# A two-layer adapter kernel on one core: new order of all engines within a step, and gathers put between the stores

## What is computed

```python
def cond(x, A, B, ids):                       # both layers
    Bx = einsum('bni,bri->bnr', x, B[ids])
    return einsum('bnr,bor->bno', Bx, A[ids])
# layer 0: c = cond(x, A0, B0, itok_B_3_7)
# x = x + c @ W0.T + b0 + sum_e alpha_e(c) * 2 * (c @ loraA_e.T) @ loraB_e.T
# layer 1: c = cond(x, A1, B1, itok_B_4_50)
# x = x + c @ W1.T + b1 + sum_e gate_e(c) * 2 * (c @ A_e.T) @ Bm_e.T
```

## Time and profile before

| | |
|---|---|
| median of 3 runs | 334.89 us (334.2 to 335.64) |
| profiled execution, its own time | 334.41 us |
| its span in the trace | 332.7 us |
| mean granted PE clock | 0.995 of full |
| PE busy | 307.0 us, 92% |
| DVE, ACT, POOL busy | 220.1, 186.4, 63.3 us |
| DMA | 56.16 MB, 169 GB/s mean |

### The profile page before, as it was taken

How to read it: one execution, slowest core, us unless ns; L and a number is a source line. 1 busy time by engine, 2 the same in 40 slices (tenths; PEclk the granted TensorE clock), 3 DMA queues, 4 the chain that set the end, 5 groups by cost and what they waited for, 6 DMA issues and landing times.

```text
span 332.7 us, 6476 instructions
## 1 busy us (share of the span) xinstructions
PE 307.0 (92%) x2048; PEld 284.4 (85%) x2048; DVE 220.1 (66%) x476; ACT 186.4 (56%) x384; POOL 63.3 (19%) x58
## 2 busy tenths in 40 slices
PE   5994998799989998999979999999999999999894
PEld 4453998589978998999979999999999999899783
DVE  2156887686738766686658666777668676864556
ACT  1446976946546565755466465646575657461520
POOL 5600000620042103320143003320332024200000
PEclk9999899999999999999999999999999999999999
DMA  7999973006870388126840587037811783041006
GB/s 267 345 365 381 347 208 156 0 8 167 300 224 0 104 243 302 51 60 212 286 139 0 158 284 250 2 103 244 299 47 55 255 292 92 0 193 62 1 0 252
DMA packets 30773, 56.16 MB, mean 169 GB/s; under 512 B 3633, under 2 KB 20050, under 8 KB 30754
## 3 DMA queue, kind: packets, MB, share of 16 engines
q1 hardware_dynamic: 29666, 52.97, 48.3%
q0 software_dynamic: 1088, 2.97, 2.5%
HBM read 39.15 MB, written 16.78 MB: 168 GB/s over the span
## 4 chain that ended last, share of the span: by engine, by line
issue 41%; PE 20%; DMA 13%; POOL 12%; DVE 6%; ACT 3%; SPq 2%; POOLq 1%; DVEq 0%; ACTq 0%
POOL xs_lo L952 8%; DMA out<-xraw 6%; DMA xraw<-x_in 6%; PE ps_d L307 3%; PE ps_d L309 3%; PE ps_d L308 3%; POOL a1s_lo L952 2%; DVE xs_lo L740 2%; DVE xraw L942 2%; PE ps_d L545 1%; PE ps_p L307 1%; PE ps_d L547 1%; ACT res L574 1%; SPq L253 1%; SPq L251 1%
## 5 line engine op out<-in xcount | busy, mean ns | idle before, releaser
L952 POOL TENSOR_TENSOR xs_lo<-xraw,xs_hi 128x512 fp32r<-128x512 f32 x28 | 36.0, 1290 | 182.5 <-ACT xs_hi L574 182.4
L307 PE MATMUL ps_d<-w1s_hi,a1s_hi 128*128 128x384 f32 (+1 forms) x192 | 63.9, 333 | 0.0
L309 PE MATMUL ps_d<-w1s_hi,a1s_lo 128*128 128x384 f32 (+1 forms) x192 | 62.0, 323 | 0.0
L308 PE MATMUL ps_d<-w1s_lo,a1s_hi 128*128 128x384 f32 (+1 forms) x192 | 61.9, 322 | 0.0
L942 DVE SCALAR_TENSOR_TENSOR xraw<-ps_d,lp,xraw 128x512 f32<-128x512 f32 x60 | 43.6, 748 | 22.5 <-PE ps_d L547 22.5
L574 ACT ACTIVATE xs_hi<-xraw 128x512 fp32r<-128x512 f32 x60 | 36.0, 626 | 26.4 <-DMA xraw<-x_in 25.9
L307 PE MATMUL ps_p<-xs_hi,bst_hi 128*128 128x256 f32 x120 | 36.5, 304 | 6.2 <-DVE bst_lo L740 2.4
L308 PEld LDWEIGHTS ps_d<-w1s_lo,a1s_hi 128*128 128x128 f32 x192 | 36.2, 189 | 0.0
L307 PEld LDWEIGHTS ps_d<-w1s_hi,a1s_hi 128*128 128x128 f32 x192 | 36.1, 188 | 0.0
L309 PEld LDWEIGHTS ps_d<-w1s_hi,a1s_lo 128*128 128x128 f32 x192 | 36.1, 188 | 0.0
L308 PE MATMUL ps_p<-xs_lo,bst_hi 128*128 128x256 f32 x120 | 34.5, 288 | 0.0
(11 more groups left out here) (227 smaller groups left out, 702.9 us busy)
## 6 DMA issues: line engine op xcount, KB each, us to landing
out<-xraw SPq DMA_DIRECT2D x31, 512.0 KB, 3.5
xraw<-x_in SPq DMA_DIRECT2D x28, 512.0 KB, 5.0
w_plain<-w SPq DMA_DIRECT2D x16, 512.0 KB, 8.9
abraw<-ab_tab SPq DMA_DIRECT2D x64, 128.0 KB, 2.1
b0raw<-b_tab SPq DMA_DIRECT2D x64, 64.0 KB, 2.0
xraw<-x_in POOLq DMA_DIRECT2D x4, 512.0 KB, 11.0
a_plain<-a SPq DMA_DIRECT2D x1, 512.0 KB, 3.6
out<-xraw SPq DMA_DIRECT2D x2, 256.0 KB, 2.7
```

The costliest lines, as they stand in the source:

```text
L307: pe.matmul(acc, lh, rh, start=first, stop=False, skip_group_check=True)
L308: pe.matmul(acc, lh, rl, start=False, stop=False, skip_group_check=True)
L309: return pe.matmul(acc, ll, rh, start=False, stop=final, skip_group_check=True)
L952: return pool.tensor_tensor(dst, whole, high.bitcast(F32), ALU.subtract)
```

## The change

The same instructions in another order, on five places.

- **PE**, steps 1 to 7: only the first three chunks of `wide(0)` stand ahead of the two transposes and `route(0)`; the other five and two chunks of part 1 stand between `route(0)` and `htx`; six chunks of part 1 between `turn()` and `query()`; all of part 2 behind `query()`. In step 0 the order of PE is as before. In the last step four result tiles (not five) stand ahead of the second `turn()`.
- **ACT**: `ht`, `he`, the exponential, `htx` and `coef_high(0)` go ahead of `wide_high(0)` and of all of `split_x`; `wide_high(1)` behind the first half of `split_x`, `wide_high(2)` behind the `cf` copies.
- **DVE**: half of `split_b` goes behind `coef_low(0)`; `ht_lo` is made inside `softmax(0)` while ACT takes the exponential; `wide_low(0)` goes behind `coef_low(0)`, `wide_low(1)` behind the `cf` low parts.
- **SP**: the 8 sequences' gathers are spread, 3, 2, 2 and 1, ahead of the four stores; the load of a chunk follows the store two chunks later instead of one.

```diff
@@ SP
                     sp.wait_ge(a_lo, g + 2)
-                    gather(picks, range(GROUP))
                 for i in range(CH - 1 if last else CH):
+                    if ahead:
+                        gather(picks, (range(0, 3), range(3, 5), range(5, 7), range(7, 8))[i])
                     sp.wait_ge(d_out, KT * g + KC * (i + 1))
...
-                    if ahead and i > 0:
-                        sp.wait_ge(stored[i - 1], 16 * g + 16)
-                        load_x(g + 2, par, i - 1)
+                    if ahead and i > 1:
+                        sp.wait_ge(stored[i - 2], 16 * g + 16)
+                        load_x(g + 2, par, i - 2)
                 if ahead:
-                    sp.wait_ge(stored[CH - 1], 16 * g + 16)
-                    load_x(g + 2, par, CH - 1)
+                    for i in (CH - 2, CH - 1):
+                        sp.wait_ge(stored[i], 16 * g + 16)
+                        load_x(g + 2, par, i)
@@ PE
                     after_step(pe, d_out, KT * g)
-                    wide(0)
+                    wide(0, range(3))
...
                 route(0, f0x)
-                if not first:
-                    wide(1)
-                wide(2, range(KT // 2))
+                if first:
+                    wide(2, range(KT // 2))
+                else:
+                    wide(0, range(3, KT))
+                    wide(1, range(2))
...
                 turn()
-                wide(2, range(KT // 2, 3 * KT // 4 if last else KT))
+                if first:
+                    wide(2, range(KT // 2, KT))
+                else:
+                    wide(1, range(2, KT))
...
                 query()
-                if last:
-                    wide(2, range(3 * KT // 4, KT))
+                if not first:
+                    wide(2)
...
-                    start_results((0, 1, 2, 3, 4))
+                    start_results((0, 1, 2, 3))
...
-                    from_layers(5)
-                    from_layers(6)
+                    for m in (4, 5, 6):
+                        from_layers(m)
@@ ACT
-                wide_high(0)
                 act.wait_ge(ht_done, g + 1)
...
-                if not last and not first:
-                    split_x(g + 1, 1 - par, 0, [0, 1])
                 softmax_exp(0)
-                wide_high(1)
...
                 coef_high(0)
+                wide_high(0)
                 if first:
                     split_b(g + 1, QUARTERS[0:2])
                 if not last:
-                    split_x(g + 1, 1 - par, 0, range(CH) if first else [2, 3])
-                wide_high(2)
-                if first:
-                    split_b(g + 1, QUARTERS[2:4])
-                if not last:
-                    split_x(g + 1, 1 - par, 1, [0])
+                    split_x(g + 1, 1 - par, 0)
+                wide_high(1)
...
                     m0x_high(0, 2, ps_h)
+                wide_high(2)
+                if first:
+                    split_b(g + 1, QUARTERS[2:4])
                 if not last:
-                    split_x(g + 1, 1 - par, 1, range(1, CH))
+                    split_x(g + 1, 1 - par, 1)
@@ DVE
                 if not last and not first:
-                    split_b(g + 1)
+                    split_b(g + 1, (0, 1))
...
+                    if layer == 0:
+                        dve.wait_ge(ht_hi, 2 * g + 2)
+                        low(ht[:, 1, :], ps_t[:, 0:P], ht[:, 0, :])
+                        low(he[ELO, :], ps_t[0:LR, P:2 * P], he[0:LR, :]).then_inc(ht_lo, 1)
...
+                softmax(0)
+                coef_low(0)
+                if not last:
+                    split_b(g + 1, (0, 1) if first else (2, 3))
                 wide_low(0)
-                dve.wait_ge(ht_hi, 2 * g + 2)
-                low(ht[:, 1, :], ps_t[:, 0:P], ht[:, 0, :])
-                low(he[ELO, :], ps_t[0:LR, P:2 * P], he[0:LR, :]).then_inc(ht_lo, 1)
-                softmax(0)
-                wide_low(1)
-                coef_low(0)
-                if first:
-                    split_b(g + 1, (0, 1))
...
+                wide_low(1)
                 if first:
                     split_b(g + 1, (2, 3))
```

## The result

The changed kernel takes 363.72 us (median of 4 runs, 361.76 to 364.52); the kernel before, run beside it, 335.26 (4 runs). The ratio is 1.085, 95% interval 1.080 to 1.089: **slower by 28 us**, where 3.0 was forecast and 342.5 was the end of the range. The direction was right, the size was not.

The account below looks back on a forecast made before the run. PE, busy 92% of the span, was taken as the bound, with at most some 25 us of stalls to win. Steps 1 to 6 +3.8, step 0 +1.4, last step -2.2 gave +3.0: 337.9 us median, range 327.5 to 342.5.

Parts of the forecast that it names:

- Step length without stalls: Steps 1 to 6: a bare step takes 34.4 us, so six take 206.4.
- When PE reaches `turn()`: In each step PE is ready for `turn()` 8.4 us after the step's first matmul, 4.5 earlier than before.
- X + 4.6: When PE can start `turn()`: 4.6 us after ACT starts the bst_hi copies, through `softmax(0)` and the subtractions.
- X: Time from a step's first matmul to ACT's start of the four bst_hi copies, which need all 16 gathers.
- What happens to X: SP's queue: last gathers wait behind a load of x, copies start at 5.6 us, bounds 3.5 to 6.0.
- both signs of being wrong: The forecast is wrong if the bst_hi copies start before 4.5 or steps 4 to 6 take less than 35.
- 10.8 + 3.1: Steps 1 to 6: waits at `turn()` of 1.8 us each, 10.8; slow issues in the first three bodies, 3.1.
- Rival 3: New waits at `turn()` drop PE's clock, two to six falls costing 3.4 to 10 us: 341 to 348; chance 0.12.
- Step 0, +1.4: ACT's new order delays the second half of `split_x`, so `project(1, 1)` starts later: 1.4 us longer, bounds 0.5 and 2.
- Last step, -2.2: All of part 2 (4.2 us) covers PE's wait of 2.07 ahead of `route(1)`: 2.2 us shorter.
- The x loads no longer count: ACT's waits for loads of x vanish: issued sooner and waited for after `coef_high(0)`.
- Rival 1: The last gathers land on time, not held by the load: X 3.5 to 4.4, 326.1 to 330.6 us; chance 0.28.

Follow-up runs that it names:

- first edit: The changed kernel with the last sequence's gathers moved ahead of the third store in SP's queue; 326.97 us, ratio 0.980 to the kernel before.
- the second: The changed kernel with the last sequence's gathers between the third store and the first load of x; 334.41 us, ratio 0.998 to the kernel before.
- the filler: The changed kernel plus 18 matmuls with unread results ahead of `htx` in steps 1 to 6; 350.5 us, ratio 1.047 to the kernel before.
- SP's program put back: The changed kernel with SP's old program (all 16 gathers, then stores and loads); 337.96 us, ratio 1.010 to the kernel before.
- SP's program alone: The kernel before with only SP's new program, other engines in their old order; 365.28 us, ratio 1.090 to the kernel before.

## Why the prediction failed, point by point

- **Step length without stalls: right.** 34.4 was forecast. The first edit has plain steps (4 to 6) of 34.3 to 34.6, and no wait at half 1 of `project` stands out in steps 1 to 6 of the changed kernel.
- **When PE reaches `turn()`: right.** Due at 8.4, and 8.34 to 8.37 wherever nothing is late.
- **X + 4.6: right.** In step 4, X is 7.9 and `turn()` starts at 12.4, X + 4.5; in step 1, 9.5 and 13.9.
- **What happens to X: wrong, the first step that failed.** That the last gathers are held by the load was forecast and is so: the one on which X hangs lands half a microsecond behind it. Not all of them queue behind it, though: in five of the six steps (3 is the exception) the 64 KB gather, issued behind the load, landed 0.3 to 0.7 ahead of it. What was wrong is the size. X is 7.9 in the plain steps and 8.7 to 9.5 in the first three, where 5.6 (6.6 with the slow issues) was forecast and 6.0 was the upper bound.
  - *The issue.* In step 4 the load is issued at S + 0.9, not 0.3, and the third store at S + 0.3, not -0.3. SP even started 0.3 sooner than in the earlier trace rows, at S - 9.0, but the 14 gathers and two stores took 9.3 us, not 8.4. In this step the second issue behind each of these two stores took 0.62, not 0.33.
  - *The landing.* The load lands 6.5 us after its issue, not 5.0. The two are together 2.1 of the 2.3; the rest is what had been taken off for an earlier start.
  - *Where the 5.0 came from.* It is the median of all loads of the kernel before, and that mixes two kinds. In its steps, the loads issued over 2 us behind the last store took 3.9 to 5.1. The one in each of six steps that went out less than 1 us behind a store took 6.2 to 6.8, and the changed kernel's is of this kind. The price stood in the trace of before (row below: the load issued at 160.07, 0.6 behind a store).
  - *Why it is so* is argued, not shown. It fits that what the store still has to move goes first: in step 4 the load lands 7.1 us after the store's issue in the change, 7.0 in the first edit and 6.9 in the second, though it is issued 0.6 behind it in the first two and 2.0 in the third. But the transfers issued behind the load are in flight with it too.
  - *The bounds and the sum.* The bounds were drawn from the same medians, so they did not hold either, and both signs of being wrong (copies before 4.5, steps under 35) looked to the fast side alone. `turn()` in the six steps is late by 77.4 - 6 x 8.4 = 27.0 us in all, against 10.8 + 3.1. The 3.1 for the slow issues of the first three steps was right: their X is above 7.9 by 3.1 in all. The 10.8 was the term that was mis-sized: it came to 23.9.

```profile
xraw<-x_in SPq DMA_DIRECT2D x1, 512.0 KB, 6.7
```

- **The clock: wrong, the second step.** Rival 3 had a chance of 0.12 and two to six falls of 1.7 us. It came in every one of the six steps, each time for about 6.8 us at half rate, not 3.4. What remains of the six steps is 246.3 - 206.4 - 27.0 = 12.9 us, 2.15 a step; with the filler this rest is 0.7. The evidence against it was real but about another size: stands of 1.73 us left the clock whole, but these are of 3 to 4.6. The second error hangs on the first: had X been 5.6, the stand would have been 1.8, and the clock perhaps whole (of the stands of 1.66 and 1.96 above, one was followed by a fall and one was not).
- **Step 0, +1.4: right** (+1.3), and for the reason given: the second half of `split_x` starts at 65.9 and `project` half 1 at 68.0, against 67.7 forecast. The fall of 3.4 us in it is not the cause: the first edit has the same order, no fall, and 42.9 us. **Last step, -2.2: right** (-2.4). The wait of 2.07 ahead of `route(1)` is gone: its first matmul follows part 2 at once.

```profile
345.79 0.34 PE L312 MATMUL ps_d<-w1s_hi,a1s_lo 128*128 128x384 f32 x1
345.97 0.20 PE L317 MATMUL ps_z<-f1s,cf 128*128 128x72 f32 x1
```

- **The x loads no longer count: right.** ACT waited 25.9 us for them before, and 2.9 in the changed kernel.
- **Rival 1** (on time) is what the first edit makes of the change. The rival had X at 3.5 to 4.4 in plain steps and 326 to 331 us; that edit measured 3.2 to 3.6 and 327.0. The rival erred only on the queue.

So the loss of 28 us is: 27.0 of lateness at `turn()`, 12.9 that is nearly all clock (0.7 of it stays with the filler), and -0.7 for step 0 and what stands ahead of it less the last step's gain (1.3 + 0.4 - 2.4), all against 216.5 - 206.4 = 10.1 of stalls that the six steps had before: 27.0 + 12.9 - 0.7 - 10.1 = 29.1, the difference of the spans.

The Trainium skill (DMA: Bandwidth & Descriptors, section "Two DMAs through the same engine are not ordered") has a later descriptor free to finish writing ahead of an earlier one. The trace agrees for the 64 KB gather of step 4, which landed 0.5 ahead of the load. It gained nothing for X, since the 128 KB one landed 0.5 behind the load.

The Trainium skill (TensorE: Matmul & The Clock Gate, Part 1) has PE fall back to half clock when it has idled. The falls in six steps of six agree, and so does the whole clock in five of six with the filler. The one shown with SP's program put back is another case: there PE had been busy 2.76 of the 4.50 us ahead of it.

## What to carry to other kernels

Ask of each DMA that someone waits for soon what is queued ahead of it, and price it by the landing of that neighbour in that place, not by a median over the kernel: the loads right behind a store took 6.2 to 6.8 us in a kernel whose median was 5.0. With two small gathers behind a store and a load of 512 KB this change cost 8%; with them ahead it saved 2%. In the same way, don't let a small urgent item (the exponential, on which PE waits) stand in an engine's program behind a large one that waits for memory. And when an estimate gives PE a new stand of a few microseconds, add what the clock takes behind it: here half as much again.

## What was not expected of the hardware

- A stand of 3 to 4.6 us in a PE that is otherwise always busy was followed by about 6.8 us at half clock, in six steps of six. The net cost was 2 us each.
- For smaller stands the runs give no simple rule. One of 1.73 us left the clock whole. A pair of 1.66 and 0.51 brought 3.4 us at half clock, and a pair of 1.96 and 0.51 in the same run brought none. The stand of 2.07 in the last step left the clock whole in the kernel before and was followed by 6.8 us at half clock with SP's program alone. With SP's program put back, three of at most 0.8 us within 4.5 us brought 3.4 us at half clock: several small waits close together can cost more than one.
- The last 128 KB gather takes 2.1 to 2.5 us ahead of the third store, 3.0 to 4.1 behind it, and 5.2 to 5.8 behind store and load.
- A load of 512 KB issued less than 1 us behind a store took 6.2 to 6.8 us in the kernel before, and 3.9 to 5.1 when issued over 2 us behind.
- The second issue behind a store took SP 0.62 to 0.66 us in the step shown, where the others take 0.33 to 0.36; the kernel before had one of 1.11 among its gathers. Why is open.
